# A graph-network layer on one core: SyncE fetches 36 source rows a pass instead of 40

## The reference

```python
h = jnp.maximum(_layernorm(x, axis=-1), 0.0)
agg = jax.ops.segment_sum(h[src], dst, num_segments=N)   # per edge: one row of h
z = (1.0 + eps_gin) * h + agg
t = jax.nn.relu(_batchnorm(jnp.dot(z, W1) + b1, g1, bt1))          # 256 -> 512
out = jax.nn.relu(_batchnorm(jnp.dot(t, W2) + b2 + h, g2, bt2))    # 512 -> 256
return x + out
```

## Time and profile before

| | |
|---|---|
| Median of three runs | 2220.45 us |
| The profiled execution's own time | 2220.37 us |
| Span, from its first to its last instruction | 2218.5 us |
| Busy: TensorE (PE) / VectorE (DVE) / ScalarE (ACT) / GpSimd (POOL) | 65% / 53% / 51% / 66% |
| Granted TensorE clock, mean | 0.816 of full |
| SyncE: 1 KB row transfers issued (`rl_odd` from `x`) | 3712 |

### The profile page before, as it was taken

One profiled execution on the slowest core, in us unless ns is written; L12 is line 12 of the kernel. 1 busy time (PEld: TensorE's weight loads), 2 busy tenths in 40 slices (PEclk: granted clock), 3 DMA queues, 4 the chain that ended last, 5 costly groups with the idle time before them and its releaser, 6 DMA issues. The chain is left out here.

```text
span 2218.5 us, 37477 instructions
## 1 busy us (share of the span) xinstructions
PE 1443.6 (65%) x4841; PEld 921.4 (42%) x4841; DVE 1183.5 (53%) x4692; ACT 1136.8 (51%) x2511; POOL 1462.8 (66%) x1559
## 2 busy tenths in 40 slices
PE   2556655666655665765766565665656566579997
PEld 2334433444433443433444344443434344354446
DVE  7455554555554555554555545555544555553346
ACT  5455554555544555554555445555445455464446
POOL 7777776777776777776777776777776777730002
PEclk7778777778887888777778887888777887799999
DMA  5334443344343344343344433434434434438447
GB/s 146 115 116 120 129 133 120 114 135 135 115 127 121 116 134 132 114 130 120 115 133 135 134 112 119 135 116 132 126 113 123 133 116 133 129 120 314 170 141 297
DMA packets 118939, 300.49 MB, mean 135 GB/s; under 512 B 33158, under 2 KB 57176, under 8 KB 112546
## 3 DMA queue, kind: packets, MB, share of 16 engines
q0 software_dynamic: 76656, 212.52, 32.0%
q1 hardware_dynamic: 39196, 84.16, 10.9%
q10 hardware_dynamic: 2838, 1.45, 0.2%
HBM read 258.75 MB, written 39.25 MB: 134 GB/s over the span
## 5 line engine op out<-in xcount | busy, mean ns | idle before, releaser
L513 POOL DMA_INDIRECT arena<-in_x,arena x1507 | 1430.7, 949 | 513.6 <-issue 441.4
L1132 PE MATMUL ps<-arena 128*96 128x256 f32 x3126 | 1002.1, 492 | 729.9 <-ACT arena L939 729.9
L939 ACT ACTIVATE arena<-arena,nb,mv 128x256 f32<-128x256 f32 x1523 | 770.6, 587 | 900.1 <-DVE nb L617 867.9
L1132 PEld LDWEIGHTS ps<-arena 128*96 128x96 f32 x3126 | 661.7, 218 | 1054.6 <-issue 790.3
L549 DVE BATCH_NORM_STATS2 st<-arena 128x6 f32<-128x256 f32 x1523 | 517.5, 412 | 728.5 <-DMA arena<-in_x,arena 590.4
L629 DVE TENSOR_TENSOR arena<-arena,ps 128x768 f32<-128x768 f32 x196 | 185.6, 947 | 4.9 <-PE ps L1132 4.8
L1161 PE MATMUL ps<-arena 128*128 128x512 f32 (+3 forms) x412 | 186.2, 577 | 2.6 <-DVE arena L737 2.6
L1241 PE MATMUL ps<-arena,W2s 128*128 128x512 f32 (+1 forms) x400 | 167.9, 582 | 0.5 <-ACT arena L1085 0.5
L535 POOL DMA_DIRECT2D out<-arena x25 | 13.5, 539 | 226.5 <-DVE arena L895 226.5
L706 DVE TENSOR_TENSOR aggT<-aggT,ps 128x192 f32 x196 | 68.5, 350 | 140.4 <-PE ps L1142 121.6
L556 DVE BATCH_NORM_AGGREGATE mv<-st 128x2 f32<-128x6 f32 x1563 | 121.4, 150 | 1.4 <-issue 0.3
(11 more groups left out here) (86 smaller groups left out, 602.0 us busy)
## 6 DMA issues: line engine op xcount, KB each, us to landing
rl_odd<-in_x SPq DMA_DIRECT2D x3712, 1.0 KB
t_T<-arena SPq DMA_DIRECT2D x24, 1024.0 KB, 13.7
arena<-t_T SPq DMA_DIRECT2D x24, 1024.0 KB, 4.9
arena<-in_x,arena POOLq DMA_INDIRECT x1507
W2s<-in_x ACTq DMA_DIRECT2D x1408, 1.0 KB
arena<-in_x SPq DMA_DIRECT2D x97, 128.0 KB
arena<-in_x SPq DMA_DIRECT2D x23, 512.0 KB, 5.8
out<-arena POOLq DMA_DIRECT2D x23, 512.0 KB, 3.8
```

What stands on the lines that cost most here:

```text
L513: nc.gpsimd.indirect_dma_start(out=rows[g % RG][:, k, :], out_offset=None, in_=x[:, :], in_offset=bass.IndirectOffsetOnAxis(ap=at, axis=0) ...
L939: last = S.activation(hrow[g % 2][:, k, :], rows_of(g, k), ACT.Relu, bias=nb[:, g % 2, k:k + 1], scale=mv[:, g % 2, k, 1:2])
L1132: last = T.matmul(win_ps[g % 2], sel[:, g % 2, k, :], hrow[g % 2][:, k, :], start=k == 0, stop=k == n - 1)
```

## The change

SP_PASS goes from 40 to 36 and SP_REGS from 20 to 18. The formulas for `sp_groups` are as they were: SyncE now has 26 tiles (3328 rows, 92.4 passes), in groups 10, 18, 24, 32, 38, 46, ... 188. GpSimd has 1526. The function that cuts a share into pieces is shared by both queues; ScalarE's pieces are the same as before (eight rows a step). The windows' first nodes, plus a half window, are written into PSUM (bank 1) instead of SBUF; the positions and the check value are formed from there.

```diff
-SP_PASS = 40
+SP_PASS = 36
 ACT_STEP = 8
 ROW_BUFS = 3
-SP_REGS = 20
+SP_REGS = 18
...
+        base_ps = ps[:, 1, 0:NG]
...
+        def row_pieces(part, each, tiles, most):
+
+            pieces, a, end = [], part * each, min((part + 1) * each, P * tiles)
+            while a < end:
+                n = min(most, end - a, P - a % P)
+                pieces.append((a // P, a % P, n))
+                a += n
+            return pieces
...
-                for j, e, n in row_pieces(c):
+                for j, e, n in row_pieces(c, SP_PASS, len(sp_groups), SP_REGS):
                     load_rows(j, e, n)
...
-            own(V.tensor_scalar(base_f, misc_ps[:, 0:NG], HALF, None, ALU.add))
+            own(V.tensor_scalar(base_ps, misc_ps[:, 0:NG], HALF, None, ALU.add))
             dve.wait_ge(s_iota, 2)
             own(V.tensor_tensor(rel_g, dst_f[:, 0:NE].rearrange("p (g k) -> p g k", k=GT),
-                                base_f.unsqueeze(2).to_broadcast([P, NG, GT]), ALU.subtract))
+                                base_ps.unsqueeze(2).to_broadcast([P, NG, GT]), ALU.subtract))
...
-            own(V.tensor_tensor(base_f, base_f, sched, ALU.subtract))
+            own(V.tensor_tensor(base_f, base_ps, sched, ALU.subtract))
...
-            def load_rows(g):
-
-                j, e = divmod((g - 1) * ACT_STEP, P)
-                if j >= len(act_groups):
-                    return
+            def load_rows(j, e, n):
...
-                load_rows(g)
+                for j, e, n in row_pieces(g - 1, ACT_STEP, len(act_groups), ACT_STEP):
+                    load_rows(j, e, n)
```

More of the change, by code:

```diff
@@ L415, in load_rows @@
                                  ).then_inc(s_sprows[j % ROW_BUFS], 16)
[L417 to L423, removed]
             sp.wait_ge(s_at, 1)
@@ L1001, in load_rows @@
                     act.wait_ge(s_actat[j % 2], 16 * (j // 2 + 1))
-                act.reg_load(regs, act_at[j % 2][0:1, e:e + ACT_STEP])
-                for k in range(ACT_STEP):
+                act.reg_load(regs[0:n], act_at[j % 2][0:1, e:e + n])
+                for k in range(n):
                     at = act.snap(regs[k], min_val=0, max_val=(N - 1) * ROW_BYTES)
```

## The result

The changed kernel took 2282.65 us (median of four runs, 2279.14 to 2284.32) beside 2219.86 us for the kernel before: a ratio of 1.028, 95% interval 1.026 to 1.030. It is 62.8 us slower; I had forecast 48 us faster.

What follows compares the result with a forecast made beforehand. SyncE was taken as the long-run limiter, GpSimd 0.54 us a pass behind it. From 2220.37 us, removing the stall (-52.2) and adding three gathers (+3.8) gave 2172.0 us, range 2165 to 2190.

Steps and rivals of the forecast that it cites:

- GpSimd's stall: Main loop: GpSimd's waits for TensorE's aggregation beyond normal issue, blamed on SyncE's slower pass; predicted to go, -52.2 us.
- the price of a register load: SyncE's pass: a load of 18 registers taken as 0.05 us less than one of 20, bounds 0 and 0.16.
- Rival E: SyncE's pass stays 20.06 us, paced by its transfers and not its instructions; 2219 us, chance 0.02.
- Three gathers more: Main loop: three tiles move from SyncE to GpSimd at 1.254 us each, +3.8 us.
- Tile by tile in time: Main loop: SyncE's rows land in time for each tile, store passes up to 2.1 us late but covered; priced 0.
- rival B: Main loop: part of the stall stays, about 22 store passes costing 0.5 to 1 us each; 2183 to 2194 us, chance 0.11.
- rival C: Main loop: the stall comes from the aggregations' own length, not SyncE, so 52.2 us stay; 2224.2 us, chance 0.03.
- Base in PSUM: Before the main loop: three VectorE instructions read an operand from PSUM at no cost; 0, bounds -0.1 and +0.2 us.
- the 1.61 us delay: One gather beside VectorE's subtraction took 2.56 us instead of 0.95; expected to go without gain, bounds -1.6 and 0.
- rival D: The gather's 1.61 us delay counts after all and the closing is quick; 2166 to 2168 us, chance 0.06.
- The wait that I had put at 3.3 us: GpSimd's wait for TensorE's first aggregation, growing from 1.68 to 3.3 us, with the loop still beginning at 47.88.
- Behind the loop: From GpSimd's last gather to W2's product, 33.5 us, nothing changes; 0, bounds 4.6 us either way.

Runs made afterwards that it cites:

- 20 + 16: The changed kernel with SP_REGS 20 instead of 18, on another chip: 2169.87 us beside 2220.88 for the kernel before, ratio 0.977.

## Why the prediction was wrong

**The reading of before was right.** SyncE sets the long-run pace, GpSimd's stall is the difference of the two passes, and 52.2 us were to be had: 20 + 16 took them.

**The step that failed** is the price of a register load: "A load of 18 lies between; I take 0.05 us less than one of 20, the bounds being 0 and a tenth of it, 0.16." Both pieces fell outside those bounds. On a 16-byte step a load of 18 took 1.58 us, 0.13 more than one of 20 where I had 0.05 less; off it, in the second piece, it took 3.94, which is 2.5 us more. I had priced the load by its length alone. All loads together took 209.4 us more, about 2.3 us a pass, where my sum took 0.1 us off. The pass came to 20.69 us, not 18.4, far above my upper end of 18.5. Everything behind that step followed: SyncE never waited, the stall grew by 61.2 us in place of falling by 52.2. Rival E had the right place, a SyncE that does not get faster, but gave it to the transfers; rows stayed 0.387 us apart (median of either trace). The range did not reach it because I bounded the load from two rows of before, both with starts on 16-byte steps. The operation that the change adds, a load from the middle of such a step, was in no row, and I did not see that it was a new one.

The Trainium skill ("Runtime: NRT & Kernel Launch", Instruction fetch mechanics) puts a TENSOR_LOAD at about 200 ns a register, on a page that speaks of registers loaded from HBM. For starts off a step the traces agree, though these loads come from SBUF (0.20); on a step they show about a quarter to a third of it (0.05 to 0.07). I had left it out, since the loads of before contradicted it (20 registers in a gap of 1.58 us).

**Other steps.** Three gathers more: +3.8 us, held (1510 at 0.946 us and 0.305 of issue). Tile by tile in time: held once the loads were quick, stall 0.5 us, so the store passes (rival B) cost nothing there. The stall is not TensorE's own (rival C): refuted, the same waits fell to issue. Base in PSUM: operand free, 1.79 us as before, the 1.61 us delay gone, and no gain to be seen (against rival D, whose 2166 to 2168 us the cut 20 + 16 did not reach either). The wait that I had put at 3.3 us with the loop's start at 47.88 was 2.82 us at 47.31 in the changed kernel and 4.86 at 49.03 with the base in PSUM alone, so its size was not forecast well, without an effect on the time. Behind the loop: GpSimd's last gather began at 2027.70 us, 59.8 us later than before, and from there to W2's product at 2064.44 it took 36.7 us, not 33.5. That is 3.2 us more, within my bounds of 4.6. Over the kernels measured at the usual speed this stretch took between 33.2 and 36.7 us without regard to the edit, so a few of the microseconds between any sum here and its measurement are its scatter. The near hit of 20 + 16 is partly luck for the same reason: its last gather began at 1915.74, 3.8 us before the 1919.5 forecast (its gathers took 945 ns each, not 949, some 6 us over 1510 of them), and its closing stretch took 35.4 us, 1.8 more than before.

## What to carry to other kernels

A size that changes how a table is cut changes addresses too: list the start of every piece, not only the lengths, and treat a start on a new alignment as an operation that the old trace does not show. Keep register loads on 16-byte starts in SBUF; there 20 registers cost less (1.39 to 1.45 us) than 6 off it (1.54). When a queue is saturated with one-row transfers, read the gaps between its rows before trusting the count of its rows.

## What the runs showed of the hardware

A load of registers from SBUF on SyncE costs about 0.35 us and 0.05 us a register when it starts on a multiple of 16 bytes, and 0.28 us and 0.20 us a register when it does not; two registers left over behind whole groups of four cost 0.4 us (18: 1.58 us, 16: 1.16 to 1.23). The first load behind a 1 MB store's issue takes some 2.1 us more, on or off a step (3.50 for 1.39, 6.39 for 4.26). And one chip took 1.4 to 1.6 times as long for each of the five kernels run on it, with holes of 0.7 us between SyncE's instructions; what makes them stays open.
